# Coupling stage: ungated state turned by three transposes per tile, gate rows multiplied in by VectorE, both sums of the output on GpSimd

## What is computed

```python
h = _layernorm(x, axis=-1) * (1 + cb) + sb
x = x + gb * _L1_ffn_ref(h, ...)

def _twist(x):
    o_r, o_i, p_r, p_i = jnp.split(x, 4, axis=-1)
    return jnp.concatenate([p_r, -p_i, -o_r, o_i], axis=-1)
out = h
for _ in range(3):
    tf = _coupling_net(out, ...)
    coupling = 0.1 + adaptive_range * (0.7 * gf + 0.3 * tf - 0.5) * 2.0
    out = out + coupling * _twist(out)
```

## Time and profile before

| | |
|---|---|
| median of 3 runs | 1158.73 us (1157.92 to 1158.9) |
| profiled execution | 1161.28 us, its span 1159.4 us, so 1.88 us lie around the span |
| busy share: PE, DVE, ACT, POOL | 89%, 63%, 52%, 41% |
| coupling stage | from about 966 us of the span to its end |
| mean granted TensorE clock | 0.949 of full speed |

### The profile page before, as it was taken

One profiled execution on the slowest core, in us unless ns is written; L12 is line 12 of the kernel. 1 busy time (PEld: TensorE's weight loads), 2 busy tenths in 40 slices (PEclk: granted clock), 3 DMA queues, 4 the chain that ended last, 5 costly groups with the idle time before them and its releaser, 6 DMA issues. The chain is left out here.

```text
span 1159.4 us, 19260 instructions
## 1 busy us (share of the span) xinstructions
PE 1029.5 (89%) x6278; PEld 578.4 (50%) x6278; DVE 726.1 (63%) x1546; ACT 601.5 (52%) x1149; POOL 474.1 (41%) x703
## 2 busy tenths in 40 slices
PE   4689899999999995599998865999999998999997
PEld 3234444444444442356565532656666664455654
DVE  1658888887888864633342223777678772565856
ACT  2248778786777774023332224434444444776752
POOL 2554546445564410268888873334333410000000
PEclk9779999999999998599999987999999998999999
DMA  5622315234152303456766761021211002001001
GB/s 164 115 47 29 77 32 106 63 75 95 42 107 48 58 30 84 148 136 134 162 150 147 193 100 28 11 62 42 78 43 42 19 16 91 1 19 55 28 28 54
DMA packets 74443, 85.81 MB, mean 74 GB/s; under 512 B 12602, under 2 KB 68674, under 8 KB 74218
## 3 DMA queue, kind: packets, MB, share of 16 engines
q1 hardware_dynamic: 61994, 67.79, 22.8%
q0 software_dynamic: 12288, 16.79, 8.6%
q10 hardware_dynamic: 64, 0.02, 0.0%
HBM read 45.26 MB, written 25.21 MB: 61 GB/s over the span
## 5 line engine op out<-in xcount | busy, mean ns | idle before, releaser
L645 DVE TENSOR_REDUCE nmax<-psum 128x1 f32<-128x512 f32 (+3 forms) x352 | 210.4, 634 | 29.5 <-PE psum L880 26.9
L767 ACT ACTIVATE pT<-psum 128x512 f32<-128x512 f32 x320 | 178.9, 596 | 40.3 <-PE psum L905 19.1
L880 PE MATMUL psum<-k6T,q6T 122*128 122x512 bf16 (+3 forms) x512 | 126.9, 315 | 24.5 <-DVE nmax L645 22.2
L1191 POOL DMA_INDIRECT residual<-expert_y,idx_e x64 | 101.3, 1584 | 26.3 <-issue 16.8
L1710 DVE TENSOR_TENSOR l_scores<-psum,const_sb 128x512 f32<-128x512 f32 x128 | 79.4, 682 | 19.4 <-PE psum L1885 19.3
L880 PEld LDWEIGHTS psum<-k6T,q6T 122*128 122x128 bf16 x512 | 43.5, 99 | 96.1 <-DVE nmax L645 72.1
L921 PE MATMUL psum<-pT,v 128*32 128x512 f32 x640 | 85.0, 604 | 0.0
L1178 POOL DMA_INDIRECT expert_tokens<-router_input,idx_e x64 | 63.2, 988 | 50.5 <-POOLq L1011 31.3
L905 PE MATMUL psum<-q6T,k6T 125*128 125x512 bf16 x192 | 71.2, 385 | 5.4 <-ACT pT L767 4.2
L1843 PE MATMUL psum<-l_hT,l_w 128*128 128x512 f32 x128 | 64.7, 629 | 1.6 <-ACT l_hT L1778 0.9
L1245 PE MATMUL psum<-expert_h,expert_w 128*128 128x512 f32 x128 | 62.1, 631 | 0.0
(11 more groups left out here) (299 smaller groups left out, 2291.5 us busy)
## 6 DMA issues: line engine op xcount, KB each, us to landing
q6T<-q_parts SPq DMA_DIRECT2D x96, 128.0 KB, 4.2
expert_w<-in_ew SPq DMA_DIRECT2D x16, 768.0 KB
x_in<-in_x SPq DMA_DIRECT2D x8, 512.0 KB, 4.1
residual<-x SPq DMA_DIRECT2D x32, 128.0 KB, 1.9
router_input<-h SPq DMA_DIRECT2D x32, 128.0 KB, 1.8
l_x<-residual SPq DMA_DIRECT2D x8, 512.0 KB
x_dram<-l_x SPq DMA_DIRECT2D x32, 128.0 KB, 1.7
out<-c_out SPq DMA_DIRECT2D x16, 256.0 KB, 2.1
```

The lines of the kernel that those rows point to most:

```text
L645: dve.tensor_reduce(nmax[:, i, u * nh:(u + 1) * nh], ps_s[:, n % SR, 0:nh * (i + 1) * P].rearrange("p (h k) -> p h k", h=nh), AX_X, ALU.ma ...
L767: act.activation(pT[:, n % PR].rearrange("p h t -> p (h t)"), ps_t[:, n % TR, :], ACT.Exp, scale=HD ** -0.5).then_inc(probs, 1)
L880: last = pe.matmul(out[:, a], q6T[0:MASK_ROWS, b % 2, u * nh + a, i * P:(i + 1) * P], keys[:, first:first + step_by * i + 1:step_by, :], s ...
L1191: pool.indirect_dma_start(out=rows, out_offset=bass.IndirectOffsetOnAxis(ap=m.idx_e[:, e, i:i + 1], axis=0), in_=y[:, e % YS, i, :], in_of ...
```

## The change

The gate is kept as rows. The routing stage computes the rows of both gates in one product of 8 x 512 and no longer the coupling gate's columns; the experts' stage finishes them on DVE, writes a signed copy with three small instructions, and stores three rows per sequence. In the coupling stage SP loads, per pair, gate row and signed row of both sequences to all partitions (two DMAs of 256 KB): those of pairs 0 and 1 first of all, those of pair q + 2 behind the last store of pair q. The step `diag` is gone. PE turns each tile with three plain transposes (channel halves 0, 1, 0), so that columns 0 to 255 are the state and 128 to 383 its halves swapped. DVE multiplies both out of psum with alpha or beta and the gate row, with no link between the two; POOL adds x and the first part, then the second part. The buffer of parts holds four tiles.

```diff
@@ routing_phase
-                for lo, hi in ((0, 4), (6, 12)):
+                for lo, hi in ((0, 4), (6, 10)):
                     act.activation(m.modT[:, 1, lo:hi, :], ps_col[:, lo:hi, :], ACT.Copy)
-                act.activation(m.gate_row[:], ps_row, ACT.Copy)
+                act.activation(m.gate_row[:, 0:2 * C], ps_row, ACT.Copy)
...
-                    pe.matmul(ps_row, m.silu[:, 1, k, :], wmod[:, k, 4 * P:6 * P], start=k == 0, stop=k == KC - 1)
+                    pe.matmul(ps_row.rearrange("b (r c) -> b r c", r=2), m.silu[:, 1, k, :],
+                              wmod[:, k, :].rearrange("p (r c) -> p r c", r=2)[:, :, 4 * P:6 * P], start=k == 0, stop=k == KC - 1)
@@ expert_phase
-                gate(m.gate_row[:], rtmp[:, 0], rtmp[:, 1]).then_inc(row_final, 1)
+                link(gate(m.gate_row[:, 0:2 * C], rtmp[:, 0], rtmp[:, 1]))
+                unsigned = m.gate_row[:, C:2 * C]
+                for lo, hi, sign in ((0, 64, 1.0), (192, 256, 1.0), (64, 192, -1.0)):
+                    ins = dve.tensor_scalar(m.gate_row[:, 2 * C + lo:2 * C + hi], unsigned[:, lo:hi], sign, None, ALU.mult)
+                ins.then_inc(row_final, 1)
...
-                link(gate(m.modT[:, 1, 10:12, :], ctmp[:, 0], ctmp[:, 1]))
@@ coupling_phase, SP
+                def load_rows(q):
+                    for a in range(2):
+                        sp.dma_start(grow[:, q % 2, a], m.mod_rows[2 * q + a:2 * q + a + 1, ROW_GATE_C * C:(ROW_SIGNED_C + 1) * C].rearrange(
+                            "b (r c) -> b r c", r=2).to_broadcast([P, 2, C])).then_inc(row_loaded[q % 2], 16)
+
+                for q in range(2):
+                    load_rows(q)
                 for s in order:
...
+                        if n == 2 * NT - 1 and q + 2 < R:
+                            sp.wait_ge(parts_ready, 2 * NT * (q + 1))
+                            load_rows(q + 2)
@@ coupling_phase, GpSimd
+                    if s[0] == "oT":
+                        _, q, n = s
+                        t = o_use[s]
+                        pool.wait_ge(first_part, t + 1)
+                        settle(pool, m.passed)
+                        link(pool.tensor_tensor(parts[:, t % 4, 2, :], x_in[q % 3][:, n, :], parts[:, t % 4, 0, :], ALU.add))
+                        pool.wait_ge(parts_ready, t + 1)
+                        settle(pool, m.passed)
+                        if q >= 2:
+                            pool.wait_ge(store[q % 2], 16 * NT * (q // 2))
+                            settle(pool, m.passed)
+                        pool.tensor_tensor(ot[:, q % 2, n, :], parts[:, t % 4, 2, :], parts[:, t % 4, 1, :], ALU.add).then_inc(done, 1)
@@ coupling_phase, VectorE
-                            dve.wait_ge(diag_ready, q)
                             dve.wait_ge(x_drain, x_use[("hT", q - 1, 1, 1)] + 1)
...
-                        dve.wait_ge(o_fill, o_use[s] + 1)
-                        if q >= 2:
-                            dve.wait_ge(store[q % 2], 16 * NT * (q // 2))
-                        link(dve.scalar_tensor_tensor(out=ot[:, q % 2, n, :], in0=ps_o[:, n % 2, 0:C], scalar=al3[:, i, a:a + 1],
-                                                      in1=x_in[q % 3][:, n, :], op0=ALU.mult, op1=ALU.add))
-                        dve.scalar_tensor_tensor(out=ot[:, q % 2, n, :], in0=ps_o[:, n % 2, C:2 * C], scalar=be3[:, i, a:a + 1],
-                                                 in1=ot[:, q % 2, n, :], op0=ALU.mult, op1=ALU.add).then_inc(done, 1)
+                        t = o_use[s]
+                        dve.wait_ge(o_fill, t + 1)
+                        if n == 0:
+                            dve.wait_ge(row_loaded[q % 2], 32 * (q // 2 + 1))
+                        if t >= 4:
+                            dve.wait_ge(done, t - 3)
+                        dve.scalar_tensor_tensor(out=parts[:, t % 4, 0, :], in0=ps_o[:, n % 2, 0:C], scalar=al3[:, i, a:a + 1],
+                                                 in1=grow[:, q % 2, a, 0, :], op0=ALU.mult, op1=ALU.mult).then_inc(first_part, 1)
+                        dve.scalar_tensor_tensor(out=parts[:, t % 4, 1, :], in0=ps_o[:, n % 2, P:P + C], scalar=be3[:, i, a:a + 1],
+                                                 in1=grow[:, q % 2, a, 1, :], op0=ALU.mult, op1=ALU.mult).then_inc(parts_ready, 1)
@@ coupling_phase, ScalarE
-                    if s[0] == "diag":
...
-                                act.activation(diag[:, q % 3, a, k, :], ident, ACT.Copy, scale=cols[:, 4 + k, a:a + 1])
-                                ins = act.activation(diag[:, q % 3, a, KC + k, :], ident, ACT.Copy, scale=sgate[:, k, a:a + 1])
@@ coupling_phase, TensorE
-                        pe.wait_ge(diag_ready, q + 1)
                         if o_use[s] >= 2:
-                            pe.wait_ge(done, o_use[s] - 1)
-                        for w in range(2):
-                            for k in range(KC):
-                                last = pe.matmul(ps_o[:, n % 2, (KC * w + k) * P:(KC * w + k + 1) * P],
-                                                 o[:, q % 3, a, 1 - k if w else k, i * P:(i + 1) * P], diag[:, q % 3, a, KC * w + k, :],
-                                                 start=True, stop=True)
+                            pe.wait_ge(parts_ready, o_use[s] - 1)
+                        for at, k in enumerate((0, 1, 0)):
+                            last = pe.transpose(ps_o[:, n % 2, at * P:(at + 1) * P], o[:, q % 3, a, k, i * P:(i + 1) * P], ident)
                         last.then_inc(o_fill, 1)
```

More of the change, by code:

```diff
@@ L974, in _ @@
                     step(s)
[L976 removed]
+MOD_COLS = (0, 1, 2, 3, 6, 7, 8, 9)
 LOWEST = -3.0e38
@@ L2014, in coupling_lead @@
     lead.xn_ready = sem("cpl_xn_ready")
+    lead.row_loaded = [sem(f"cpl_gate_rows_loaded{s}") for s in range(2)]
     lead.x3_store = [sem(f"lin_x3_stored{s}") for s in range(2)]
```

46 lines of the change are left out of this document (14 added, 32 removed).

## The result

The changed kernel took 1168.6 us (median of 4 runs, 1165.98 to 1169.16) against 1158.33 us for the kernel before beside it (4 runs): a ratio of 1.0092, 95% interval 1.0072 to 1.0112. Measured again beside the experiments it was 1.0074 (1.0054 to 1.0093). So it is slower by 9 to 11 us; 1167.0 was forecast, in a range of 1161.0 to 1174.5.

A forecast was written before the change was run, and what follows sets the result against it. PE was taken to bound most of the coupling stage, then DVE, then the tail; -8 (PE) + 4 (updates) + 3 (load) + 3 (DVE's stretch) + 6.3 (tail) = +8.3 on 1158.7, so 1167.0 us, range 1161.0 to 1174.5.

The forecast's parts named there:

- PE's saving: Coupling stage turns: three instructions per tile instead of eight, at most 11.1 us in PE's stretch, 8 us after normalization waits.
- tail: Last eight tiles of pair 3: POOL's two linked sums set a 1.79 us pace per tile, +6.3 us.
- load for pair 3: Load behind POOL's last sum of pair 0 and two row loads: 4 us later, charged 3 us (1 to 5).
- updates held, pairs 0 and 1: DVE's SBUF updates in PE's stretch wait for POOL's sums: 2 us lost per pair (0 to 4), +4.
- DVE's stretch: 1119.8 to 1133.5 us, where DVE's updates set the chain: nine POOL sums fall there, 3 us lost (about 1 to 4.4).
- The alternation: DVE's SBUF updates beside POOL's sums: either only first waits, 0.4 us per tile group, or alternating, 0.73 us per sum.
- the sign: Evidence named for a right forecast: L2195 to L2205 on DVE with maxima of 1.3 us and more, mean before 0.69.
- (a): Pairs 0 to 2 in PE's stretch: PE's saving outruns the tail, kernel faster, -1.7 to -4.8 us; 4% with (d).
- (b): Whole kernel: balance within 0.2%, gain 8 and other charges 2 or 3, given as +0.5 to +2 us; 8%.
- (c): Around each pair's first tiles: PE's pauses let its granted clock fall, +5 to +8 us on top, 1173 to 1176; 15%.
- (d): Tail: POOL isn't paced by the links, the tail ends with DVE at 7.7 us plus one POOL tile; 1%, within (a).
- The small parts: Diagonals, wider row product, longer row gate and first four row loads: nothing, or 1 to 2 us if cover were gone.

The follow-up runs named there:

- e4: Kernel before with the ungated state turned by three transposes per tile, no diagonals, gate and sign left out, no sums or row loads; ratio 0.9947 to before.
- e10: Changed kernel with a fourth buffer for x, so the load for pair 3 waits for no sum of pair 0; ratio 1.0042 to before.
- e9: Kernel before plus one POOL sum of 128x512 from constants behind each tile of the first three pairs, nobody waiting for it; ratio 1.0043 to before.
- e2: Changed kernel without POOL sums in the first three pairs, whose outputs lack x and the first part; ratio 1.0028 to before.
- e8: Kernel before plus two linked POOL sums of 128x256 from constants behind each tile of the first three pairs, nobody waiting; ratio 1.0031 to before.
- e1: Changed kernel with one POOL sum instead of two per tile in the last pair, whose output lacks its second part; ratio 1.0025 to before.
- e3: Changed kernel with a gate-row buffer per pair, all row loads issued behind the load of x for pair 2; ratio 1.0055 to before.
- e6: Kernel before with DVE multiplying the state by gate columns ahead of the turn, four plain transposes per tile, no diagonals, sums or row loads; ratio 0.9932 to before.
- e5: Kernel before plus the change's row loads at the change's places, into a buffer that nothing reads; ratio 0.9997 to before.
- e12: e6 with the last pair's tiles turned into four psum banks instead of two; ratio 0.9949 to before.

## Why the prediction was right

The sign, the size and the largest term were right. Two of the other terms were each off by about 3 us, in opposite directions: that the sum came within 1 us (+8.3 for +9.21) is luck. With the load alone put right the forecast would have been 1170, with the held updates alone 1164, both still in the range.

| step | forecast | measured |
|---|---|---|
| PE's saving | -8 | -7.36 (e4 against before), some 1.0 of it in the tail |
| tail | +6.3 | +6.05 in all; the sums cost 7.08 (e4's tail to the changed one's), the turn gave 1.0 |
| load for pair 3 | +3 | +6.30 (e10 against changed) |
| updates held, pairs 0 and 1 | +4 | +1.43 (e10 against e4, pair 0 to pair 2) |
| DVE's stretch | +3 | +2.25 (the same, pair 2 to pair 3) |
| sum | +8.3 | +9.21 (changed against before; the rows above give 9.70, as pair 0 itself came 0.5 us earlier in e10 than in e4) |

**PE's saving.** A transpose at half a product held: six in 0.85 us in the changed kernel, (0.85 - 0.27) / 5 = 0.116 each. That the normalization eats part of it also held: in e4 PE waits 1.13 us for it before its next transposes, twice in PE's stretch, where I had 1.5. Of at most 11.1 us 6.33 arrived before the tail. That the five tiles beside DVE's chain give nothing was right (pair 2 to pair 3 took 32.60 us in e4, 32.21 before); that the eight of the tail give nothing was wrong: in a tail with DVE as the pace a quicker turn gives about 1.0 us.

**The tail.** Right in its pace and its end: cycle 1.78 us for 1.79, pause 0.37 for 0.36, last sum done at 1163.95 for 1163.0, from a first scaling 1.15 us later than I started it. DVE waited for POOL only from the seventh tile on and not from the fifth, since the four buffers let it run ahead further than I had counted. The estimate by the Trainium skill's 2.6 cycles per element (GPSIMD Engine Reference, section 3.1), +3.4 us, is too low; the row's 0.73 us per sum decided it. e9 tells how the two differ: 512 elements take 1.27 us and 256 take 0.73, so 0.54 us for each 256 and 0.19 at the start. By the elements alone the page's figure agrees: 0.54 us for 256 is 2.5 cycles each at its 1.2 GHz.

**The load.** The mechanism was right (behind POOL's last sum, behind two row loads, `fin` and pair 1 behind it on DVE), its size wrong. The step that failed is "0.5 MB ahead of its 1 MB, I add 1.5". It was 3.4: 9.0 us from issue to statistics instead of 5.6. With POOL's lag and SP's issues, 3.4 us more between DVE's last scaling and the issue (3.9 for 0.5), the load landed 6.8 us later behind DVE's last scaling of pair 0, where I had 4. At +6.30 us the term lies outside its own bounds, 1 to 5, and 3.4 outside the 0 to 2.8 of that step. Beyond the slack each of these microseconds counts in full, and it brought a pause of PE with it: with the clock at 0.79 behind it, eight projections took 1.14 us more.

**The alternation.** The open question was whether a row of DVE's operations goes through as one. It does not: they alternate, the upper bound of the two. In DVE's stretch that came to 2.25 us for my 3, by e10 against e4, which had the same granted clock there (0.89 and 0.90). The size isn't fixed better than to 2 us: against e2 (0.93) it is 3.8, and in the kernel before 3.7 (e9) to 4.2 (e8). The longest 128x512 products took 1.23 us, a little less than the 1.3 that I had named as the sign. In pairs 0 and 1 it came to 1.43 for my 4: the delays were there, as the averages of 0.87 and 1.53 us show, but they fell where PE was the bound (e8 and e9 lose only 0.9 us there). The step that failed is "some 12 of the 16 sums fall near them, and I take 2 us lost per pair": it took being near for being on the path, with only 1 us of slack allowed.

**Rivals.** (a), that PE's saving outruns the tail, fell: it needed no charge before the tail, and there were 9.5 us. (b) fell with it. (c) happened in part: the clock fell behind the wait at 1074 us and was lower at 1135 to 1140 us (0.52, and eight instructions of layer 2 in 5.84 us for 5.37), together 1.6 us, not 5 to 8. From pair 0 to pair 3 the mean granted clock was 0.957, in the kernel before 0.986; I estimate from it that the falls of the clock together cost at most 3.6 us more than before, (1 - 0.957) x 121.8 - (1 - 0.986) x 118.0, and only if PE had been the bound throughout. (d) fell with e1. Two of the rivals' sums are slips: (b) should read +0.3 to +1.3 (-8 + 6.3 + 2 or 3), and (c) 1172 to 1175 (1167.0 + 5 to 8); neither touches the forecast.

**The small parts.** Routing and experts' stage: no sign of them, as forecast. The four row loads ahead of the load for pair 1 made its statistics wait 11.72 us instead of 6.59, and e3, where they don't, has pair 0 in the same place (63.50 for 63.09 us): nothing, as forecast.

## What to carry to other kernels

Work moved to an idle engine costs what its own cycle is where nothing runs beside it (the tail), and what the busy engine loses in sharing SBUF with it elsewhere; look first for idle time on the engine that already touches the data, as e6 did. For a transfer, note how much slack lies behind it on the waiting engine's own list: below that a delay is all but free, as in e5, above it all of it counts, and two causes of the same delay don't add up when taken away one at a time. Count from the start of the stage that is changed; of the spread between executions some 4 us came from the stages ahead.

## What the runs showed of the hardware

**The load.** Two broadcast loads of 256 KB with 2 KB per partition, issued just ahead of a load of 1 MB, made it 3.4 us slower (e3 against changed: 5.4 and 9.0 us from issue to the first use), in the kernel before 2.1 us (e5: 7.7 against 5.6). Why the two differ no run shows.

**The clock in the tail.** Stretches of the tail, the kernel before, then e4, then e12:

```profile
1148.00:1152.00 4.00, 2.69 (x22) 2.56 (x23) 3.46 (x8) 0.00 (x0) 0.00 (x0) 1.00 0.19 66
```
```profile
1139.00:1143.00 4.00, 3.42 (x12) 2.01 (x12) 3.69 (x9) 0.00 (x0) 0.00 (x0) 0.50 0.21 66
```
```profile
1140.00:1143.00 3.00, 1.94 (x18) 1.70 (x17) 2.32 (x12) 0.27 (x1) 0.00 (x0) 1.00 0.00 0
1143.00:1147.00 4.00, 3.10 (x16) 1.97 (x16) 3.86 (x10) 0.00 (x0) 0.00 (x0) 0.80 0.26 90
```

With products between the scalings the granted clock was 1.00, with three transposes 0.50 (1.2 GHz), in e6 with four as well. In e4 six transposes took 1.81 us there, for 0.85 just ahead of the tail at the upper level (2.4 GHz). So the quicker turn of the tail ran at half speed and still gave its 1.0 us. The Trainium skill, TensorE: Matmul & The Clock Gate, Part 4, says that the full clock doesn't engage for transposes. e4 fits that, but in e12 sixteen of them ran at 1.00 without a break; and PE had paused 2.24 us ahead of e4's second group and 2.12 ahead of e6's, against 1.15 in the kernel before and 1.24 in e12. Whether it was the kind of work or the pause that let the clock fall no run here separates.
